# Histogram steps by Sign on ScalarE, late gathers, run marks stored as rows, and the first power pass's loads on ScalarE's queue

## The reference, cut to what matters

```python
# L0: edge network, messages summed at their destination
h = relu(edge_attr @ W1.T + b1); w = h @ W2.T + b2
agg = segment_sum(w * x[src], dst, N)
x = layernorm(x + relu(x @ Ws.T + bs + agg @ Wn.T + bn))
# L1: 10 power steps over the edges turned round
w = rsqrt(max(deg_row, 1)[row] * max(deg_col, 1)[col])
for _ in range(10): out = segment_sum(out[col] * w, row, N) * 0.9 + x * 0.1
x = layernorm(x + out / theta)
# L2: 16 smoothing steps with self loops; L3: two graph convolutions with PReLU
...
```

## Time and profile before

| | us |
|---|---|
| median of three runs (8792.99 to 8802.09) | 8794.96 |
| the profiled execution's own time | 8794.6 |
| span of its trace | 8792.5 |
| busy: POOL / PE / DVE / ACT | 6478.6 / 5522.7 / 4914.3 / 2041.9 |

### The profile page before, as it was taken

One profiled execution on the slowest core, in us unless ns is written; L12 is line 12 of the kernel. 1 busy time (PEld: TensorE's weight loads), 2 busy tenths in 40 slices (PEclk: granted clock), 3 DMA queues, 4 the chain that ended last, 5 costly groups with the idle time before them and its releaser, 6 DMA issues. The chain is left out here.

```text
span 8792.5 us, 112510 instructions
## 1 busy us (share of the span) xinstructions
PE 5522.7 (63%) x24034; PEld 4418.1 (50%) x24034; DVE 4914.3 (56%) x12173; ACT 2041.9 (23%) x5604; POOL 6478.6 (74%) x6812
## 2 busy tenths in 40 slices
PE   7676835555555543347777777777776667766643
PEld 6565723333333332226666666656555555655533
DVE  7688736555556566645555555544444444465544
ACT  2355832111111113533111111100000000065433
POOL 6666767777777777677777777777777777777777
PEclk9777855555555555557877777777667666666555
DMA  7665564444444433323444444433333333333211
GB/s 143 130 163 155 148 128 128 113 113 112 113 112 117 115 106 109 110 70 113 121 112 115 114 114 113 113 105 101 96 99 98 98 98 98 103 94 88 81 45 37
DMA packets 955827, 954.11 MB, mean 109 GB/s; under 512 B 426114, under 2 KB 846716, under 8 KB 955046
## 3 DMA queue, kind: packets, MB, share of 16 engines
q1 hardware_dynamic: 696366, 602.87, 22.8%
q0 software_dynamic: 217408, 320.06, 16.7%
q10 hardware_dynamic: 41370, 23.99, 1.1%
HBM read 565.09 MB, written 409.02 MB: 111 GB/s over the span
## 5 line engine op out<-in xcount | busy, mean ns | idle before, releaser
L1996 POOL DMA_INDIRECT l_g<-tab,marks x3094 | 2922.8, 945 | 951.4 <-issue 870.6
L2214 DVE TENSOR_TENSOR_SCAN l_w<-l_m,l_w,bank 96x512 f32<-96x512 bf16 x1248 | 1591.4, 1275 | 2620.5 <-PE bank L2028 2610.7
L2028 PE MATMUL bank<-ident,l_g 128*96 128x128 f32 x5030 | 1165.3, 375 | 1627.7 <-DMA l_g<-tab,marks 914.3
L1996 POOL DMA_INDIRECT l_g<-tab,XM x1740 | 1648.2, 947 | 541.4 <-issue 476.3
L2028 PEld LDWEIGHTS bank<-ident,l_g 128*96 128x96 f32 x5030 | 755.0, 171 | 2073.9 <-DMA l_g<-tab,marks 1030.3
L2048 PEld LDWEIGHTS bank<-ident,l_w 96*128 96x128 f32 x6272 | 1603.7, 328 | 327.9 <-issue 256.4
L2048 PE MATMUL bank<-ident,l_w 96*128 96x96 f32 x6272 | 1508.9, 403 | 10.2 <-DVE l_w L2214 10.2
L2039 PE MATMUL bank<-XM,ident 128*128 128x384 f32 x1568 | 921.4, 681 | 0.0
L2118 ACT ACTIVATE T<-T,marks 128x96 f32<-128x96 f32 x196 | 57.0, 362 | 1967.1 <-DVE T L2239 1966.7
L309 PE MATMUL bank<-tail_xt,v 96*96 96x500 f32 (+1 forms) x298 | 275.7, 1026 | 319.9 <-ACT tail_xt L304 319.9
L420 ACT ACTIVATE tail_y<-bank,tail_of,tail_sc 125x96 f32<-125x96 f32 (+1 forms) x596 | 208.2, 429 | 1095.3 <-DVE tail_of L411 1083.4
(11 more groups left out here) (334 smaller groups left out, 9352.2 us busy)
## 6 DMA issues: line engine op xcount, KB each, us to landing
tab<-T SPq DMA_DIRECT2D x828, 192.0 KB
row_buffer<-tab ACTq DMA_DIRECT2D x5808, 0.4 KB
tab<-l_o SPq DMA_DIRECT2D x441, 192.0 KB
l_m<-mask_d SPq DMA_DIRECT2D x784, 96.0 KB
l_g<-tab,marks POOLq DMA_INDIRECT x3094
l_m<-mask_s SPq DMA_DIRECT2D x490, 96.0 KB
row_buffer<-tab SPq DMA_DIRECT2D x2640, 0.4 KB
l_g<-tab,XM POOLq DMA_INDIRECT x1740
```

The costliest lines, as they stand in the source:

```text
L1996: nc.gpsimd.indirect_dma_start(out=tile(G[q % RG], t), out_offset=None, in_=tables[0:table_at + (2 - p % 2) * TR, :] if p else first, in_o ...
L2028: last = nc.tensor.transpose(a_bank(q)[0:D, u:GE:U], rows[:, u * D:(u + 1) * D], self.ident[:, :])
L2214: v.tensor_tensor_scan(out=W[q % RW][:, :], data0=masks[q % RM][:, :], data1=a_bank(q)[0:D, :], initial=W[(q - 1) % RW][:, GE - 1:GE] if q ...
```

## The change

1. The low one-hot table of the destinations becomes a step table: ScalarE writes sign(number - digit + 0.5), four tiles at once, one group ahead (`low_steps`), between the snapshot and the rectifier. The destination histogram then holds cumulative counts in another form, and `node_records` gets the counts by differences in place of a scan.
2. The edge groups are taken in reverse. Nine of the 49 (LATE) are gathered later: five groups by GpSimd in `node_records`, four at the beginning of `rank_edges`. Their edge weights are kept in XM and multiplied in `rank_edges`. The pacing waits of GpSimd's gathers are gone.
3. The marks are transposed on TensorE and stored as 49 rows of 1 KB. The first four own-row gathers move from `prepare` into the power passes.
4. `load_head` of power pass 0 is issued by ScalarE instead of SyncE.

```diff
@@ histograms
+    def fetch_sources(self, pool, first, groups):
+        for k, n in enumerate(groups):
+            q, g = first + k, NGP - 1 - n
+            if self.groups + q >= AHEAD_GROUPS:
+                pool.wait_ge(self.fills(q - AHEAD_GROUPS), self.full(q - AHEAD_GROUPS))
+            for t in range(g * U, (g + 1) * U):
+                self.nc.gpsimd.indirect_dma_start(
+                    out=self.T[:, t * D:(t + 1) * D], out_offset=None, in_=self.i["x"],
+                    in_offset=bass.IndirectOffsetOnAxis(ap=self.src_i[:, t:t + 1], axis=0),
+                ).then_inc(self.fills(q), 16)
...
-                for g in range(NGP):
-                    if g >= PACE:
-                        pool.wait_ge(split, g - PACE + 1)
...
+                self.fetch_sources(pool, 0, SOON)
...
-                            last = v.tensor_scalar(ol[k][t % R8][:, :], iota_lo[:, :], lo[k][:, t:t + 1], None,
-                                                   ALU.is_equal)
+                        v.tensor_scalar(ol[0][t % R8][:, :], iota_lo[:, :], lo[0][:, t:t + 1], None,
+                                        ALU.is_equal).then_inc(onehot, 1)
...
+                    if n in LATE:
+                        v.tensor_copy(self.late_weights(LATE.index(n)), edge_out[:, 0:GD]).then_inc(G["gated"], 1)
+                        return
...
                     for t in range(g * U, (g + 1) * U):
                         pe.wait_ge(onehot, t + 1)
+                        pe.wait_ge(stepped, t + 1)
...
+                def low_steps(g):
+                    for t in range(g * U, (g + 1) * U):
+                        a_.activation(ol[1][t % R8][:, :], iota_lo[:, :], ACT.Sign, bias=lo[1][:, t:t + 1]
+                                      ).then_inc(stepped, 1)
...
                     a_.activation(snap[g % SK][:, 0:2 * HW], hist[0], ACT.Copy).then_inc(rounded, 1)
+                    if g + 1 < NGP:
+                        low_steps(g + 1)
                     if g:
                         rectify(g - 1)
@@ rank_edges
+                self.fetch_sources(pool, LATE_FIRST - len(LATE), LATE[LATE_FIRST:])
...
+                        pool.wait_ge(gated, len(LATE))
...
-                        if q * NT // (NGP + BOTH_FIRST) > PACE * U:
-                            pool.wait_ge(nears, q * NT // (NGP + BOTH_FIRST) - PACE * U)
...
+                def gate(k):
+                    q, g = k - len(LATE), NGP - 1 - LATE[k]
+                    dve.wait_ge(self.fills(q), self.full(q))
+                    c = slice(g * GD, (g + 1) * GD)
+                    v.tensor_tensor(out=T[:, c], in0=self.late_weights(k), in1=T[:, c], op=ALU.mult).then_inc(gated, 1)
...
+                    if m in LATE:
+                        pe.wait_ge(gated, LATE.index(m) + 1)
@@ node_records
+                self.fetch_sources(pool, len(SOON) - NGP, LATE[0:LATE_FIRST])
...
+                        link(v.tensor_copy(tot[:, :], counts[:, LO - 1:M:LO]))
+                        for h in range(2):
+                            link(v.tensor_scalar(end[:, halves[h]], counts[:, halves[h]], tot[:, h:h + 1], 0.5, ALU.add,
+                                                 ALU.mult))
...
@@ prepare
-                pool.wait_ge(indexed, 1)
-                self.fetch_own(pool, range(OWN_SOON))
...
-                        sp.dma_start(slots_of(self.mask_s[1:TR + 1]), by_group(cont[:, :])).then_inc(self.order_masked, 16)
+                    sp.dma_start(self.mask_s[1:TR + 1].rearrange("(g q) -> g q", q=GE), cont_row[:, :]
+                                 ).then_inc(self.order_masked, 16)
...
+                pe.wait_ge(linked, 1)
+                for u in range(U):
+                    last = nc.tensor.transpose(cont_turn[0:NGP, u:GE:U], cont[:, u:NT:U], self.ident[:, :])
+                last.then_inc(across, 1)
...
+                dve.wait_ge(across, 1)
+                v.tensor_copy(cont_row[:, :], cont_turn[0:NGP, :]).then_inc(rowed, 1)
@@ passes
+                def load_head(g):
+                    if g >= RG:
+                        step(act, 0, g - RG)
+                    act.dma_start(G[g % RG][:, :].rearrange("p (u d) -> p u d", d=D),
...
                 if power:
                     act.wait_ge(begun, 1)
+                    for g in range(RG):
+                        load_head(g)
...
                                 for n in backs(g):
                                     begin_total(n)
+                                if g + RG < NGP:
+                                    load_head(g + RG)
```

More of the change, by code:

```diff
@@ L55 @@
 REC_AT = 8192
-PACE = 2
+LATE = tuple(range(4, NGP, 5))
+SOON = tuple(n for n in range(NGP) if n not in LATE)
+LATE_AT, LATE_FIRST = 12288, 5
 SR = 3
@@ new lines, in _ @@
+                    dve.sem_inc(totals, 1)
+                    if k:
+                        upto = end[:, :].rearrange("p (h m) -> p h m", h=2)
+                        each = deg[k][:, :].rearrange("p (h m) -> p h m", h=2)
+                        link(v.tensor_copy(each[:, :, 0:1], upto[:, :, 0:1]))
+                        link(v.tensor_tensor(out=each[:, :, 1:LO], in0=upto[:, :, 1:LO], in1=upto[:, :, 0:LO - 1],
+                                             op=ALU.subtract))
+                    dve.wait_ge(offs, k + 1)
@@ new lines, in _ @@
+                    link(v.tensor_copy(off[:, :], self.bank[2 + k][0:HP, 0:1]))
+                    if k == 0:
+                        link(v.tensor_scalar(end[:, :], cum[:, :], off[:, 0:1], -1.0, ALU.add, ALU.add))
+                    else:
+                        link(v.tensor_copy(both[:, 0:1], off[:, :]))
+                        link(v.tensor_tensor(out=both[:, 1:2], in0=off[:, :], in1=tot[:, 0:1], op=ALU.add))
+                        for h in range(2):
+                            link(v.tensor_scalar(end[:, halves[h]], end[:, halves[h]], both[:, h:h + 1], -1.0, ALU.add,
+                                                 ALU.add))
@@ L1483, in order_out @@
                 def order_out():
-                    sp.wait_ge(linked, 1)
-                    with nc.allow_non_contiguous_dma(reason="four numbers of each partition"):
-                        sp.dma_start(slots_of(self.mask_s[1:TR + 1]), by_group(cont[:, :])).then_inc(self.order_masked, 16)
+                    sp.wait_ge(rowed, 1)
+                    sp.dma_start(self.mask_s[1:TR + 1].rearrange("(g q) -> g q", q=GE), cont_row[:, :]
+                                 ).then_inc(self.order_masked, 16)
                 with nc.allow_non_contiguous_dma(reason="one number"):
@@ L1897, in own_tiles @@
             def own_tiles(p):
-                return range(OWN_FIRST + (p - 1) * OWN if p else OWN_SOON, OWN_FIRST + p * OWN)
+                return range(OWN_FIRST + (p - 1) * OWN if p else 0, OWN_FIRST + p * OWN)
             def own_count(k, end):
@@ L2467, in _ @@
                                              ).then_inc(stored[q % RO].sem, 16)
-                            if power and p == 0 and g + RG < NGP:
-                                load_head(g + RG)
                             if looped:
```

81 lines of the change are left out of this document (42 added, 39 removed).

## The result

The changed kernel takes 8956.69 us (median of three, 8950.16 to 8957.77) against 8794.96: a ratio of 1.018 (95% interval 1.0157 to 1.0203), 162 us slower. The forecast was 8935.

| from, to | before | after | difference | forecast |
|---|---|---|---|---|
| start, 49th snapshot | 278.37 | 436.08 | +157.7 | +142 |
| to the first scatter of edge records | 603.7 | 611.0 | +7.3 | +7 |
| to the last scatter | 256.1 | 257.2 | +1.1 | 0 |
| to the first gather of power pass 1 | 214.8 | 196.4 | -18.3 | -8.5 |
| to the end | 7439.6 | 7447.8 | +8.1 | 0 |

A forecast was written before the change was run, and what follows sets the result against it. The prediction took a loop of waits between ScalarE and TensorE to bound the first stage. Its terms, 142 + 5 + 2 - 15.5 + 1 + 6 = +140.5 on 8794.6 us, gave 8935 us, range 8838 to 8980.

The forecast's parts named there:

- The bound: First stage: a loop of waits between ScalarE and TensorE sets it, 4.72 us a group, 7.42 at the lower clock.
- A Sign's price: First stage, ScalarE between snapshot and rectifier: 0.38 us a Sign, 1.53 us a group; the ends are 1.06 and 2.28.
- The clock: First stage: TensorE waits about 2.5 us a group for the rectifier, so the clock falls; 85% of groups low.
- the first term: First stage, Signs on ScalarE: 48 steps take 410 us instead of 268.17, +142.
- the clock holds as now: Rival, first stage: Signs lengthen the loop but the clock falls no more often; +72, 8866 us; chance 0.15, half way included.
- the rival by which GpSimd sets the stage: First stage: a group takes its four gathers' 4.98 us, 36 fewer give 45 us; 8748 us; chance 0.07.
- Late gathers: 36 of 196 gathers leave the first stage, worth nothing there: +5 in the node records, +2 in the ranking stage.
- Marks as rows: End of edge preparation: the 20.0 us hole becomes 2 of transposes plus 2.5 of tail, -15.5 us.
- Loads on ScalarE: Power pass 0: loads issued by ScalarE delay the first scan and take ScalarE time; +1 and +6, SyncE gains nothing.
- the +1 and the +6: Power pass 0: +1 us for a later first scan, +6 for a quarter of 22 us of load issues on ScalarE.
- the floor of GpSimd's 132 gathers: Power pass 0: 2.75 + 132 x 1.24 = 167 us into the block, against 169.3 before for pass 1's first gather.
- The rest: From the first gather of power pass 1 on: nothing that sets the time is touched, 7440 us taken as unchanged.

## Why the prediction was right, step by step

**The bound.** Right: the loop of snapshot, rectifier, product, copy and hidden layer set the stage. Signs moved out of it cost nothing, Signs put into the untouched kernel cost everything.

**A Sign's price.** Taken as 0.38 us; measured 0.496 for one and 1.69 for four, so (1.69 - 0.496) / 3 = 0.398 each, 1.59 a group instead of 1.53. The estimate by the Trainium skill ("ScalarE: Activation LUTs", section "What ACT_TABLE_LOAD costs"), 0.40, was the better one: its sum for one Sign, 280 + 0.833 x 256 = 493 ns, stands beside 496 here.

**The clock.** Right in kind: with 2.4 to 2.6 us of waiting in each group the clock falls again and again, and with the wait filled to 0.56 us it is 1.00 throughout. Off in size: the prediction took whole groups for low or full, 85% of them low. By the granted clock of 0.58 the low level did hold for 84% of the time from 100 us on. But no group ran at the full level from end to end (none is below 8.25 us), for that level came back mostly while TensorE waited, where it shortens nothing. In one such stretch TensorE is busy 1.00 of 3.50 us, and its wait of 2.50 us for the rectifier lies inside; in six of them together it is busy 5.27 of 20.60 us. Busy times of that stretch, and below them its line of the timeline:

```profile
94.10:97.60 3.50, 1.00 (x9) 0.74 (x7) 0.57 (x1) 2.66 (x6) 2.59 (x4) 0.99 1.41 145
96.86 1.41 PE L851 MATMUL bank<-w2a,XM 97*128 97x96 f32 x8 [2.50 <-ACT XM L904]
```

So the steps count as 92% low: 8.80 on the mean between 6.31 us (the step with the clock held) and 9.00. Over 47 steps that is 0.075 x 2.69 x 47 = 9.4 us of the 15.7 that the first term was too low, and the steps' own lengths (9.00 and 6.31 instead of 8.95 and 6.25) make 2.4. The other 3.9 are the start: the prediction counted the first step like the rest, which puts the second snapshot at 10.20 + 8.54 = 18.74 us, and it came at 22.62. Before it had come at 21.54. The first Signs wait 5.0 us for the digits of the destinations, but that they make the 1.1 us is not shown: kernels without Signs there have their second snapshot at 21.5 to 22.2.

The rival "the clock holds as now" drew on the Trainium skill's "TensorE: Matmul & The Clock Gate", section "HAM oscillation — how this bites in real kernels", which tells of a clock lost in long waits for data between bursts. A clock that comes and goes is what the changed kernel shows, but with waits of 2.4 to 2.6 us for the rectifier, which that rival took for harmless. That rival fell, as did the rival by which GpSimd sets the stage.

**Late gathers.** Forecast +5 in the node records and +2 in the ranking stage; the trace shows +7.3 and nothing, so that the sum came out right by luck. From the last snapshot to the first work of the ranking stage it takes 38.91 us instead of 31.59. GpSimd's 20 late gathers last 27.10 us there, 1.36 each and not 1.245, and the next stage begins 2.63 us behind the last of them, when VectorE has long been done:

```profile
471.41 0.94 POOL L566 DMA_INDIRECT T<-in_x_dram,src_i  x1 [0.30 <-issue]
474.98 0.29 POOL L998 IOTA iota_high<- 128x196 bf16 x1 [2.63 <-POOLq L1333]
```

From there to the first scatter it takes 572.08 us instead of 572.06. In the nine profiles with late gathers the node records' part takes 38.9 to 42.1 us, in the five without 30.1 to 38.8. "Worth nothing" inside the first stage was right for the changed kernel: its steps take 8.80 us, and 8.79 with all gathers in the stage.

**Marks as rows.** Forecast -15.5, as 2 us of transposes and 2.5 of tail in place of 20.0. Transposes and copy made the way from the marks' comparison to the last arithmetic 2.4 us longer (8.71 instead of 6.34), and the tail fell to 0.28, which makes -17.3. Alone the rows gave -17.2 us from last scatter to pass 1 against the profile of the kernel before (15.7 on the mean of all profiles) and a ratio of 0.9983. The four gathers had nothing to do with the hole.

**Loads on ScalarE.** This term failed: the +1 and the +6 did not come. The first scan did come later, 11.1 us into the block instead of 9.7, and 2.2 later behind the first gather than with SyncE's loads; but no time was lost by it at the end of the pass. The text had named the floor of GpSimd's 132 gathers (167 us into the block) and then put a quarter of ScalarE's issues on top. Pass 1 began 168.9 us into the block, which is that floor with 1.26 us a gather instead of 1.24 (132 in 166.1 us, without a gap). The loads have room beside it.

**The rest.** 7439.6 became 7447.8 us, which I had as unchanged. In twelve experiment profiles that stretch takes 7435.8 to 7453.4 us without any order by what was changed in them, so the 8.1 us can't be put down to the change.

**The sum.** In the profile 155.9 us came where 140.5 were forecast. The terms missed by more than that: +15.7 for the Signs, +0.3 and +1.1 up to the last scatter, +8.1 in the rest, against -9.8 for marks and loads. That the misses partly cancel is luck; that one term outweighs the others and had its cause right is not.

## What to carry to other kernels

An instruction is priced by its place before its length: 1.6 us a group on ScalarE cost some 157 us, more than half of it in clock, inside the loop that paced the stage, and nothing a few lines further down. Before moving work to an engine that looks idle, find which of its instructions another engine waits for, and put the new ones behind those. When a step moved out of a loop leaves the other engine without a wait, look at once for what is late next: here it was the gathers, then a store in small pieces.

## What the runs showed of the hardware

The kernel that gave TensorE 24 useless matmuls a group was 125 us faster than the one without them: a wait of 2.4 us in each group is also paid for in the clock (granted 0.58 instead of 1.00), a wait of 0.99 us is not. And stores in pieces of four two-byte numbers hurt beyond their own end: the issue of the next store on SyncE's queue took 10.71 us behind one (0.34 with rows of 1 KB), and 20.0 us passed at the end of a block behind the other (0.28 and 0.66 us with rows).
